# Expert weights loaded two chunks at a time, their low parts written over the raw weights, and the transposes of the gated rows moved

## The chip, the cores and the metric

The kernel runs on 1 core of one Trainium2 chip. The metric is the device time of one execution in microseconds; the median of 3 runs of the kernel before is 2552.89 us (2551.38 to 2554.53). TensorE (PE) multiplies, ScalarE (ACT), VectorE (DVE) and GpSimd (POOL) do element work, and SyncE (SP) issues most of the transfers. Sixteen DMA engines move the data.

## The reference

Two layers over a graph of 625 nodes with 1024 features. Each layer adds a graph product and a kernelized attention to x, then a mixture of experts. The change is in the mixture of experts of the first layer:

```python
def _mlp(h, wg, wu, wd):
    return jax.nn.silu(h @ wg) * (h @ wu) @ wd
...
C = int(np.ceil(CAP_FACTOR * NK / E))          # 98 rows an expert; E = 16, K = 2, F = 1408
expert_inputs = jnp.zeros((E, C, d), x.dtype).at[idx_flat, pos_c].add(x_pair)
expert_outputs = jax.vmap(_mlp)(expert_inputs, w_gate, w_up, w_down)
gathered = expert_outputs[idx_flat, pos_c] * (vals_flat * within)[:, None]
output_tokens = gathered.reshape(N, K, d).sum(axis=1)
return x + _mlp(x, sw_gate, sw_up, sw_down) + output_tokens.reshape(b, s, d)
```

wg and wu are 1024 x 1408 an expert, wd is 1408 x 1024, all in float32. One expert's three matrices are 17.3 MB (3 x 1024 x 1408 x 4 bytes), 16 experts 277 MB. `sw_*` is the shared expert, which all 625 rows pass.

## The kernel before

A float32 product is made of three TensorE products in the type fp32r: every operand is split into a high part (a rounded copy, by ACT, `a_high`) and a low part (what is left, by DVE, `v_low`), and high x high, high x low and low x high are summed in PSUM (`mm_high`, `mm_low`).

The weights come in chunks of 128 rows of the contracted dimension. A chunk of wg or wu is 128 x 1408 (704 KB, rows of 5632 bytes), one of wd, of the shared expert and of all other matrices 128 x 1024 (512 KB). An expert has 8 chunks of wg, 8 of wu and 11 of wd. The list `Weights.all` has all chunks of the program in the order of use, in four regions; region 1 is the experts. Each chunk passes three steps:

1. SP issues its DMA into a raw buffer. Region 1 has five of them, `er0` to `er4`; a buffer is taken again when the low part of the chunk five places before is made (`c.raw_over`, line 733 on).
2. ACT copies it to the high half of a slot, `es0` to `es2`, and DVE makes the low half of the same slot from raw and high. A slot is free when the product of the chunk three places before is done (`a_place`). ACT and DVE work up to three chunks ahead (`due`).
3. TensorE makes its products: for wg and wu three pieces of 512, 512 and 384 columns times three parts, 9 matmuls; for wd two pieces times three parts, 6 matmuls.

`t_experts` sets the order on TensorE. For expert x it is: gate product (`t_up` of wg); the transposes of the gated rows of expert x-1 (`t_turn`, 11 of them); up product (`t_up` of wu); the transposes of the tokens of expert x+1 (`t_enter`, 8 of them); down product of expert x-1 (`t_down`); and for x < 12 one unit of the shared expert (`t_unit`; gate and up units turn 8 weight pieces, down units go block by block). After expert 15 come its transposes, its down product and the last six units. ACT and DVE have matching lists (`a_experts`, `v_experts`). ACT applies silu to the gate product and writes `eg` (line 2041); DVE multiplies it by the up product into `eh` (`v_product`, line 2173), which `t_turn` reads. `a_turned` and `v_turned` split the transposed rows into `heT_h` and `heT_l`.

PSUM has 8 banks, given out in turn (`Banks.take`): the gate product takes 3, the transposes 3, the up product 3, so the up product takes one bank of the gate product of the same expert and waits until silu has read it.

The experts' inputs are scattered to `scr_ei` by POOL (line 2193) and read back expert by expert (`xin`); the outputs go to `scr_eo` (`a_down`), are gathered by POOL after the last expert (line 2211), and DVE adds them to x (`v_combine`). The first chunks of region 1 wait, in `a_place`, for that scatter to land, since their slots lie over rows that it reads.

## Time and profile before

| what | us |
|---|---|
| median of 3 runs | 2552.89 (2551.38 to 2554.53) |
| span of the profiled execution | 2546.2 |
| PE busy | 2453.1 (96%) |
| DVE busy | 1815.8 (71%) |
| ACT busy | 1424.6 (56%) |
| POOL busy | 631.0 (25%) |

The profiled execution has no time of its own beside its span; the median of the runs is 6.7 us over the span, which is what lies around it (start and end of the launch). The experts lie at about 430 to 1315 us. In the page's 40 slices these are the ones in which the DMA engines are 90% busy or more and move 317 to 360 GB/s. A matmul's row says how long it was under way; matmuls overlap, so what a stage costs is read from the starts of its matmuls. The granted TensorE clock is at 9 tenths or more in every slice.

### The profile page before, as it was taken

The page shows a single profiled execution, that of the slowest core. Times are in us where ns is not written, and L with a number is a line of the kernel's source. Part 1 is how long each engine was busy: PE and PEld are TensorE (multiplying, and loading weights), DVE is VectorE, ACT ScalarE, POOL GpSimd, SP SyncE. Part 2 cuts the span into 40 slices and gives each one's busy share as a digit, 9 for nine tenths or more (in the row PEclk, how much of TensorE's full clock was granted, in tenths as well). Part 3 has the DMA queues.
Part 4 walks back from the last instruction along what each step waited for, and adds up shares of the span by engine and source line. Part 5 has one row for each costly group of instructions (what it writes and reads, how often), then busy time and mean ns, then how long its engine had stood idle before and what let it go on. Part 6 is the DMA issues. An engine that isn't in the chain of part 4 may idle for free.

```text
span 2546.2 us, 32572 instructions
## 1 busy us (share of the span) xinstructions
PE 2453.1 (96%) x12692; PEld 2015.9 (79%) x12692; DVE 1815.8 (71%) x2006; ACT 1424.6 (56%) x1890; POOL 631.0 (25%) x538
## 2 busy tenths in 40 slices
PE   7999999999999999999999999999999989999999
PEld 6978798776777777776777778887899987777797
DVE  7449655878787888778868876556666768887453
ACT  5337433766676766667753344443377758885131
POOL 5858215333221000000011004443000006556000
PEclk9999999999999999999999999999999999999999
DMA  5334027999999999999985445444311138885212
GB/s 172 80 100 126 7 83 219 332 334 317 345 321 333 335 326 332 332 341 360 358 272 158 131 132 160 130 125 133 121 58 44 46 110 271 277 280 162 92 55 74
DMA packets 174096, 508.18 MB, mean 200 GB/s; under 512 B 30220, under 2 KB 48025, under 8 KB 173944
## 3 DMA queue, kind: packets, MB, share of 16 engines
q1 hardware_dynamic: 124520, 418.01, 47.3%
q0 software_dynamic: 34928, 74.92, 10.6%
q10 hardware_dynamic: 14496, 13.17, 1.6%
q8 instruction: 101, 1.65, 0.3%
q14 instruction: 51, 0.42, 0.1%
HBM read 458.93 MB, written 46.88 MB: 199 GB/s over the span
## 4 chain that ended last, share of the span: by engine, by line
PE 74%; DVE 12%; DMA 7%; ACT 3%; issue 2%; POOL 1%; SPq 0%; DVEq 0%; ACTq 0%
PE ps L204 72%; DVE es_l L243 4%; DMA er<-in_wd 2%; DVE od L235 2%; ACT es_h L767 1%; DVE Aw L231 1%; DMA gr<-scr_y,gidx 1%; DVE x L231 1%; DMA wk<-in_Wk 1%; DMA scr_ei<-xn,sdi 1%; PE ps L1997 1%; PE ps L1209 1%; DVE eh L231 1%; POOL scr_ei L2193 0%; DVE ws_l L243 0%
## 5 line engine op out<-in xcount | busy, mean ns | idle before, releaser
L243 DVE TENSOR_TENSOR es_l<-er,es_h 128x1408 fp32r<-128x1408 f32 (+1 forms) x455 | 651.8, 1446 | 174.0 <-ACT es_h L767 169.4
L767 ACT ACTIVATE es_h<-er 128x1408 fp32r<-128x1408 f32 (+1 forms) x455 | 562.9, 1242 | 247.8 <-PE ps L204 136.6
L767 ACT ACTIVATE ws_h<-wr 128x1024 fp32r<-128x1024 f32 (+1 forms) x105 | 110.1, 1051 | 205.0 <-PE ps L204 197.0
L243 DVE TENSOR_TENSOR ws_l<-wr,ws_h 128x1024 fp32r<-128x1024 f32 (+1 forms) x103 | 128.6, 1249 | 113.5 <-ACT ws_h L767 113.1
L204 PE MATMUL ps<-es_h,xe_h 128*98 128x512 f32 (+1 forms) x768 | 205.9, 376 | 2.2 <-ACT es_h L767 1.8
L204 PE MATMUL ps<-es_l,xe_h 128*98 128x512 f32 (+1 forms) x768 | 205.4, 376 | 0.8 <-DVE es_l L243 0.2
L204 PE MATMUL ps<-es_h,xe_l 128*98 128x512 f32 (+1 forms) x768 | 204.8, 375 | 0.0
L2199 POOL DMA_DIRECT2D xin<-scr_ei x16 | 9.4, 590 | 627.5 <-PE ps L1969 612.0
L204 PEld LDWEIGHTS ps<-es_l,xe_h 128*98 128x98 f32 x768 | 124.6, 163 | 41.2 <-DVE es_l L243 4.1
L204 PEld LDWEIGHTS ps<-es_h,xe_h 128*98 128x98 f32 x768 | 123.5, 163 | 41.6 <-ACT es_h L767 3.4
L204 PEld LDWEIGHTS ps<-es_h,xe_l 128*98 128x98 f32 x768 | 125.2, 163 | 37.9
L3025 POOL DMA_INDIRECT wrow<-scr_inv,gdst x96 | 110.4, 1150 | 154.6 <-DVE B_l L243 93.1
L2311 POOL DMA_INDIRECT gr<-scr_y,gidx x96 | 122.9, 1280 | 103.2 <-PE ps L204 79.1
L1178 POOL DMA_INDIRECT scr_edges<-dat,idx x85 | 122.6, 1443 | 25.9 <-issue 25.9
L204 PE MATMUL ps<-ws_h,T_h 128*125 128x512 f32 x320 | 127.7, 399 | 0.0
L243 DVE TENSOR_TENSOR T_l<-T,bh 128x1024 fp32r<-128x1024 f32 x64 | 78.2, 1225 | 68.8 <-ACT bh L2823 68.8
L239 DVE SCALAR_TENSOR_TENSOR gl<-gr,gw,gh 128x1024 fp32r<-128x1024 f32 x96 | 120.4, 1279 | 9.1 <-ACT gh L2274 9.0
L204 PE MATMUL ps<-ws_h,T_l 128*125 128x512 f32 x320 | 126.8, 396 | 0.0
L204 PE MATMUL ps<-ws_l,T_h 128*125 128x512 f32 x320 | 126.8, 396 | 0.0
L2274 ACT ACTIVATE gh<-gr,gw 128x1024 fp32r<-128x1024 f32 x96 | 109.9, 1145 | 23.3 <-PE ps L204 13.3
L204 PE MATMUL ps<-es_h,heT_h 128*98 128x512 f32 x352 | 112.8, 402 | 10.3 <-ACT es_h L767 10.2
L204 PE MATMUL ps<-T_h,ws_h 128*128 128x314 f32 x528 | 122.0, 310 | 0.7 <-DVE ws_l L243 0.7
(476 smaller groups left out, 6258.8 us busy)
## 6 DMA issues: line engine op xcount, KB each, us to landing
er<-in_wg SPq DMA_DIRECT2D x128, 704.0 KB, 6.7
er<-in_wu SPq DMA_DIRECT2D x128, 704.0 KB, 6.3
er<-in_wd SPq DMA_DIRECT2D x176, 512.0 KB, 5.2
B<-in_rel SPq DMA_DIRECT2D x64, 512.0 KB, 3.4
scr_y<-y SPq DMA_DIRECT2D x45, 448.0 KB
wr<-in_Wqkv SPq DMA_DIRECT2D x16, 512.0 KB, 5.5
wr<-in_gate SPq DMA_DIRECT2D x16, 512.0 KB, 3.5
wr<-in_w SPq DMA_DIRECT2D x13, 512.0 KB, 3.4
```

Source lines behind the costliest of these rows:

```text
L204: return e.matmul(out, l, r, start=start, stop=stop, skip_group_check=True)
L231: return e.tensor_tensor(out, x, y, op)
L235: return e.tensor_scalar(out, x, s1, s2, op0) if op1 is None else e.tensor_scalar(out, x, s1, s2, op0, op1)
L239: return e.scalar_tensor_tensor(out=out, in0=x, scalar=s, in1=y, op0=op0, op1=op1)
L243: return e.tensor_tensor(lo, src, hi.bitcast(F32), ALU.subtract)
L767: q.e.activation(c.hi, c.at, ACT.Copy).then_inc(*self.s("high").up(c.key))
L1178: q.e.indirect_dma_start(self.d_edges, to, self.m["dat2"][0:TP, 4 * c:4 * c + 4], None).then_inc(*self.landed("edges").up(c))
L1209: ins = e.transpose(ps.one(bs[k // 4], 128, (k % 4) * TP, TP), buf[t][:, k * 128:(k + 1) * 128], self.ident[0:TP, 0:TP])
L1997: ins = q.e.transpose(ps.one(bs[f // 4], 128, (f % 4) * C0, C0), self.m["eh"][0:C0, f * 128:(f + 1) * 128], self.ident[0:C0, 0:C0])
L2274: q.e.activation(m[f"gh{c % NH}"], m[f"gr{c % NR}"], ACT.Copy, scale=m["gw"][:, c:c + 1]).then_inc(*self.s("rows_high").up(c))
L2311: e.indirect_dma_start(m[f"gr{c % NR}"], None, self.d_y[:, :], of).then_inc(*self.landed(f"rows{c % NR}").up(c))
L3025: e.indirect_dma_start(m["wrow"][:, c * 8:(c + 1) * 8], None, self.d_inv[:, :], of).then_inc(*self.landed("row_weights").up(c))
```

## The change

- Two neighbouring chunks of an expert's matrix come in one transfer (`add_two`), from weights laid out so on the host (`by_two`): rows of 11264 bytes for wg and wu and of 8192 bytes for wd, 1408 KB and 1024 KB a transfer. The eleventh chunk of wd comes alone (`wd_last`). The raw buffers `pr0` to `pr4` hold two chunks each.
- The low part is written over the raw chunk (`pr_l` is the same memory). So a raw buffer is taken again only when the products of both its chunks are done. The slots `hs0` to `hs2` hold the high part alone and lie elsewhere; the first use of two of them waits for another thing than before, and no longer for the scatter.
- The transposes of the gated rows of expert x-1 stand in the gate product of expert x, ahead of its fifth chunk (`k == 4`), those of expert 15 in the down product of expert 14, ahead of its ninth chunk. `eh` is gone: DVE multiplies in place in `eg`.
- Expert 15 gets a unit of the shared expert (the 13th of the interleaved ones), so it stands ahead of the last down product, and five units follow the last down product instead of six.
- `eo` is one buffer. All other matrices that were read as two half rows of 2048 bytes are laid out on the host as rows of 4096 bytes (`quarters`, `by_half`); their transfers keep their size.

The diff, cut:

```diff
@@ -161,8 +164,32 @@
         self.of[key] = len(self.all)
         self.all.append(Chunk(key, src, n, region, **how))
 
+    def add_two(self, keys, src, n, region):
+
+        self.add(keys[0], src, n, region, with_it=keys[1:])
+        self.add(keys[1], src, n, region, part=1)
+
+    def place_loads(self, raws, highs):
+
+        mine = [c for c in self.all if c.region == 1]
+        last_in, held, load = {}, {}, -1
+        for i, c in enumerate(mine):
+            if not c.part:
+                load += 1
+                c.raw = raws[load % len(raws)]
+                c.raw_over = last_in.get(c.raw)
+            else:
+                c.raw = raws[load % len(raws)]
+            last_in[c.raw] = c
+            c.slot = highs[i % len(highs)]
+            c.over, held[c.slot] = held.get(c.slot), c
+            at = slice(c.part * c.n, (c.part + 1) * c.n)
+            c.at, c.lo, c.hi = self.m[c.raw][:, at], self.m[c.raw + "_l"][:, at], self.m[c.slot][:, 0:c.n]
+        self.last_in = last_in | held
+
     def place(self, raws, rings):
-        for r in range(4):
+        self.place_loads(raws[1], rings[1])
+        for r in (0, 2, 3):
             mine = [c for c in self.all if c.region == r]
...
@@ -316,10 +338,11 @@
             at(f"wr{i}", W + 16384 + i * 4096, 1024)
         for i in range(KD):
             at(f"wk{i}", R1 + i * 4096, 1024)
-        for i in range(3):
-            pair(f"es{i}", (R1 + 4096, R1 + 15360, W)[i], 1408)
-        for i in range(5):
-            at(f"er{i}", R1 + 26624 + i * 5632 if i < 2 else W + 11264 + (i - 2) * 5632, 1408)
+        for i, o in enumerate((R1 + 4096, R1 + 15360, R1 + 26624, W, W + 11264)):
+            at(f"pr{i}", o, 2 * F0)
+            at(f"pr{i}_l", o, 2 * F0, F32R)
+        for i, o in enumerate((U + 14144, R3 + 26816, W + 22528)):
+            at(f"hs{i}", o, F0, F32R)
 
         for i in range(5):
...
@@ -568,15 +589,16 @@
         u = 14
 
         def downs(e):
-            for f in range(FB):
-                W.add(("wd", e, f), a["wd"][e, f * 128:(f + 1) * 128, :], 1024, 1)
+            for i in range(FB // 2):
+                W.add_two([("wd", e, 2 * i), ("wd", e, 2 * i + 1)], a["wd"][e, i], 1024, 1)
+            W.add(("wd", e, FB - 1), a["wd_last"][e], 1024, 1)
         for e in range(E0):
             for n in ("wg", "wu"):
-                for k in range(KD):
-                    W.add((n, e, k), a[n][e, k * 128:(k + 1) * 128, :], F0, 1)
...
                 self.s_bias(q)
-            if c.raw_over:
+            if c.part:
+                continue
+            if c.raw_over and c.region == 1:
+                q.wait_ge(self.s("product"), c.raw_over.key)
+            elif c.raw_over:
                 q.wait_ge(*self.low(c.raw_over.key))
-            elif c.region == 1 and c.raw in ("er0", "er1"):
+            elif c.region == 1 and c.raw in ("pr0", "pr1", "pr2"):
                 q.wait_ge(self.s("aggregated"), T - 1)
             elif c.region == 1:
                 q.wait_ge(self.s("product"), self.last0)
                 q.wait_ge(*self.low(self.last0))
             elif c.region == 2:
-                q.wait_ge(*self.low(self.last1))
+                for n in {"wr0": ("pr4",), "wr1": ("pr4", "hs2"), "wr2": ("hs2",)}[c.raw]:
+                    q.wait_ge(self.s("product"), self.W.last_in[n].key)
             elif c.region == 3:
                 q.wait_ge(self.s("product"), ("block", 8, 3))
-            dst = c.at.rearrange("p (k c) -> p k c", k=c.src.shape[1]) if len(c.src.shape) == 3 else c.at
-            e.dma_start(dst, c.src).then_inc(*self.landed(c.raw).up(c.key))
+            dst = m[c.raw][:, 0:c.src.shape[1]] if c.region == 1 else c.at
+            e.dma_start(dst, c.src).then_inc(*self.landed(c.raw).up(c.key, *c.with_it))
         ov = self.out.rearrange("(t p) d -> p t d", p=TP)
...
@@ -777,12 +803,13 @@
             q.wait_ge(self.s("summed"), (NW - 1, 1))
         elif c.region == 3:
             q.wait_ge(self.s("product"), ("block", 8, {"ws0": 4, "ws1": 12}[c.slot]))
-        elif c.region == 1 and c.slot != "es2":
-            q.wait_ge(self.s("x_plus_xn"), T - 1)
-            q.wait_ge(self.landed("placed"), 2 * T - 1)
-        elif c.region and c.slot:
-            q.wait_ge(self.s("product"), self.last0 if c.region == 1 else self.last_es2)
-            q.wait_ge(*self.low(self.last0 if c.region == 1 else self.last1))
+        elif c.region == 1:
+            q.wait_ge(self.s("product"), ("swg", 0))
+            if c.slot == "hs2":
+                q.wait_ge(*self.low(self.last0))
+        elif c.region == 2 and c.slot:
...
@@ -1943,17 +1970,14 @@
         u = 14
         for x in range(E0):
             self.t_up(q, "wg", x)
-            if x:
-                self.t_turn(q, x - 1)
             self.t_up(q, "wu", x)
             if x < E0 - 1:
                 self.t_enter(q, x + 1)
             if x:
                 self.t_down(q, x - 1)
-            if x < E0 - 4:
+            if x < E0 - 4 or x == E0 - 1:
                 self.t_unit(q, u)
                 u += 1
-        self.t_turn(q, E0 - 1)
         self.t_down(q, E0 - 1)
         for i in range(u, len(self.units)):
             self.t_unit(q, i)
...
@@ -1977,6 +2001,8 @@
         for j in range(2):
             q.wait_ge(*ps.done(("enter", x), j, "low"))
         for k in range(KD):
+            if n == "wg" and x and k == 4:
+                self.t_turn(q, x - 1)
...
@@ -2005,6 +2031,8 @@
         for j in range(3):
             q.wait_ge(*ps.done(("turn", x), j, "low"))
         for f in range(FB):
+            if x == E0 - 2 and f == 8:
+                self.t_turn(q, E0 - 1)
             c = self.W.all[self.W.of["wd", x, f]]
             L = tuple(self.m["heT_" + j][:, f * C0:(f + 1) * C0] for j in "hl")
...
@@ -2030,34 +2058,36 @@
                     self.a_entered(q, 0, j)
             self.a_unit(q, i)
         u = 14
-        for x in range(E0 + 1):
-            if x < E0:
-                for k in range(KD):
-                    self.a_high(q, ("wg", x, k))
-                for i, (a, b) in enumerate(UPS):
-                    q.wait_ge(self.s("product"), ("wg", x, KD - 1))
-                    if x:
-                        q.wait_ge(*ps.done(("wu", x - 1), 2))
-                    e.activation(m["eg"][0:C0, a:b], ps.one(ps.group["wg", x][i], C0, 0, b - a), ACT.Silu).then_inc(*ps.out(("wg", x), i))
-                for k in range(KD):
-                    self.a_high(q, ("wu", x, k))
-                    if x and k < 3:
-                        self.a_turned(q, x - 1, k)
-            else:
-                for k in range(3):
-                    self.a_turned(q, x - 1, k)
+        for x in range(E0):
+            for k in range(KD):
+                self.a_high(q, ("wg", x, k))
+                if x and k > 4:
+                    self.a_turned(q, x - 1, k - 5)
+            for i, (a, b) in enumerate(UPS):
+                q.wait_ge(self.s("product"), ("wg", x, KD - 1))
+                if x:
+                    q.wait_ge(self.s("turned_hidden"), x - 1)
+                e.activation(m["eg"][0:C0, a:b], ps.one(ps.group["wg", x][i], C0, 0, b - a), ACT.Silu).then_inc(*ps.out(("wg", x), i))
+            for k in range(KD):
+                self.a_high(q, ("wu", x, k))
             if x:
                 for f in range(FB):
                     self.a_high(q, ("wd", x - 1, f))
                     if 3 <= f < 5 and x < E0 - 1:
                         self.a_entered(q, x + 1, f - 3)
+                if x == E0 - 1:
+                    for j in range(3):
+                        self.a_turned(q, x, j)
                 self.a_down(q, x - 1)
             else:
                 for j in range(2):
                     self.a_entered(q, 1, j)
-            if x < E0 - 4:
+            if x < E0 - 4 or x == E0 - 1:
                 self.a_unit(q, u)
                 u += 1
+        for f in range(FB):
+            self.a_high(q, ("wd", E0 - 1, f))
...
-                    if x and k < 3:
-                        self.v_turned(q, x - 1, k)
-            else:
-                for k in range(3):
-                    self.v_turned(q, x - 1, k)
+        for x in range(E0):
+            for k in range(KD):
+                self.v_low(q, ("wg", x, k))
+                if x and k > 4:
+                    self.v_turned(q, x - 1, k - 5)
+            for k in range(KD):
+                self.v_low(q, ("wu", x, k))
             if x:
                 for f in range(FB):
                     self.v_low(q, ("wd", x - 1, f))
-                    if f < 3 and x < E0:
+                    if f < 3:
                         self.v_product(q, x, f)
                     if 3 <= f < 5 and x < E0 - 1:
                         self.v_entered(q, x + 1, f - 3)
+                if x == E0 - 1:
+                    for j in range(3):
+                        self.v_turned(q, x, j)
             else:
                 for i in range(3):
                     self.v_product(q, 0, i)
                 for j in range(2):
                     self.v_entered(q, 1, j)
-            if x < E0 - 4:
+            if x < E0 - 4 or x == E0 - 1:
                 self.v_unit(q, u)
                 u += 1
...
@@ -2168,9 +2199,7 @@
         a, b = UPS[i]
         q.wait_ge(self.s("product"), ("wu", x, KD - 1))
         q.wait_ge(*ps.done(("wg", x), i))
-        if x:
-            q.wait_ge(self.s("turned_hidden"), x - 1)
-        tt(q.e, m["eh"][0:C0, a:b], ps.one(ps.group["wu", x][i], C0, 0, b - a), m["eg"][0:C0, a:b], ALU.mult).then_inc(*ps.out(("wu", x), i))
+        tt(q.e, m["eg"][0:C0, a:b], ps.one(ps.group["wu", x][i], C0, 0, b - a), m["eg"][0:C0, a:b], ALU.mult).then_inc(*ps.out(("wu", x), i))
 
     def v_combine(self, q, t):
...
+        return W.reshape(k, 128, 2, 512).transpose(2, 1, 0, 3).reshape(2, 128, k * 512)
+
+    def by_two(W):
+        e, k, n = W.shape
+        return W.reshape(e, k // 256, 2, 128, n).transpose(0, 1, 3, 2, 4).reshape(e, k // 256, 128, 2 * n)
+
     cst = np.zeros((128, 128 + NT), np.float32)
```

What stands in each engine's program, in the places that matter. First TensorE, expert 3, before: the last chunk's low products of the gate product (`xe` are the expert's rows, `es` the weights' slots), the 11 transposes, the first chunk of the up product.

```order
L204 MATMUL ps<-es_l,xe_h 98x512 [waits low]
L204 MATMUL ps<-es_l,xe_h 98x512
L204 MATMUL ps<-es_l,xe_h 98x384
L1997 MATMUL ps<-cst,eh 128x98 [waits bank3_emptied,bank2_emptied,bank1_emptied]
L1997 MATMUL ps<-cst,eh 128x98 x10
L204 MATMUL ps<-es_h,xe_h 98x512 [waits bank6_emptied,high,bank5_emptied,bank4_emptied]
L204 MATMUL ps<-es_h,xe_h 98x512
```

The same gate product after the change, at its fifth chunk:

```order
L231 MATMUL ps<-pr_l,xe_h 98x512 [waits low]
L231 MATMUL ps<-pr_l,xe_h 98x512
L231 MATMUL ps<-pr_l,xe_h 98x384
L2023 MATMUL ps<-cst,eg 128x98 [waits bank3_emptied,bank2_emptied,bank1_emptied]
L2023 MATMUL ps<-cst,eg 128x98 x10
L231 MATMUL ps<-hs_83,xe_h 98x512 [waits high]
```

And at its end, where the up product follows at once:

```order
L231 MATMUL ps<-pr_l,xe_h 98x512 [waits low]
L231 MATMUL ps<-pr_l,xe_h 98x512
L231 MATMUL ps<-pr_l,xe_h 98x384
L231 MATMUL ps<-hs_81,xe_h 98x512 [waits bank6_emptied,high,bank5_emptied,bank4_emptied]
L231 MATMUL ps<-hs_81,xe_h 98x512
```

The transposes no longer stand between the two products; the up product's wait for `bank6_emptied`, which is a bank of the gate product, is the same.

SP's program in region 1, after the change: the loads of the down product of expert 0, a unit, and the next gate product. Each waits for the product of the second chunk of the pair in its buffer.

```order
L771 DMA pr_71<-in_wd 128x2048 [waits product]
L771 DMA pr_73<-in_wd 128x2048 [waits product]
L771 DMA pr_75<-in_wd 128x2048 [waits product]
L771 DMA pr_77<-in_wd 128x2048 [waits product]
L771 DMA pr_79<-in_wd 128x2048 [waits product]
L771 DMA pr_71<-in_wd_last 128x1024 [waits product]
L771 DMA pr_73<-in_swu 128x1024 [waits product]
L771 DMA pr_75<-in_wg 128x2816 [waits product]
```

Before, each of these was a DMA of one chunk that waited for a low part:

```order
L745 DMA er_78<-in_wd 128x1024 [waits low]
L745 DMA er_79<-in_wd 128x1024 [waits low]
L745 DMA er_80<-in_wd 128x1024 [waits low]
L745 DMA er_81<-in_wd 128x1024 [waits low]
L745 DMA er_77<-in_wd 128x1024 [waits low]
```

A chunk's load thus moved from "low part five chunks back" to "product of a load five loads back". ACT's first three copies of region 1, before:

```order
L767 ACTIVATE es_h<-er_77 128x1024 [waits landed_placed,x_plus_xn,landed_er0]
L767 ACTIVATE es_h<-er_78 128x1024 [waits landed_er1]
L767 ACTIVATE es_h<-er_79 128x1024 [waits low,product,landed_er2]
```

and after:

```order
L793 ACTIVATE hs_81<-pr_71 128x1024 [waits landed_pr0]
L793 ACTIVATE hs_82<-pr_73 128x1024 [waits landed_pr1]
L793 ACTIVATE hs_83<-pr_75 128x1024 [waits low,landed_pr2]
```

The wait for `landed_placed`, the scatter of the experts' inputs, is gone from the first of them.

## Rows read from the trace of the kernel before

**Rows 1.** The page's first line.

```profile
span 2546.2 us, 32572 instructions
```

**Rows 2.** Timeline of PE at edges of stages: start us, us, instruction, [idle <-releaser].

```profile
470.86 0.80 PE L204 MATMUL ps<-es_h,xe_h 128*98 128x512 f32 x3
...
1092.94 0.81 PE L204 MATMUL ps<-es_h,xe_h 128*98 128x512 f32 x3
...
1141.49 0.80 PE L204 MATMUL ps<-es_h,xe_h 128*98 128x512 f32 x3
...
1291.77 1.09 PE L1997 MATMUL ps<-cst,eh 98*128 98x98 f32 x11
1297.55 0.72 PE L204 MATMUL ps<-es_h,heT_h 128*98 128x512 f32 x1 [4.69 <-ACT es_h L767]
...
1314.52 0.53 PE L204 MATMUL ps<-T_h,es_h 128*128 128x314 f32 x2
...
1367.36 0.72 PE L1209 MATMUL ps<-cst,lnx 125*128 125x125 f32 x5 [3.15 <-ACT lnx L1227]
```

**Rows 3.** Timeline of PE, the edges inside the round of expert 5.

```profile
698.41 0.80 PE L204 MATMUL ps<-es_h,xe_h 128*98 128x512 f32 x3
...
713.72 1.09 PE L1997 MATMUL ps<-cst,eh 98*128 98x98 f32 x11
714.62 0.85 PE L204 MATMUL ps<-es_h,xe_h 128*98 128x512 f32 x3
...
729.97 0.84 PE L1969 MATMUL ps<-cst,xin 98*128 98x98 f32 x8
730.59 0.69 PE L204 MATMUL ps<-es_h,heT_h 128*98 128x512 f32 x2
...
747.28 0.53 PE L204 MATMUL ps<-T_h,es_h 128*128 128x314 f32 x2 [0.59 <-DVE es_l L243]
...
754.35 0.81 PE L204 MATMUL ps<-es_h,xe_h 128*98 128x512 f32 x3
```

**Rows 4.** Timeline of PE, second and seventh chunk of a down product.

```profile
675.74 0.63 PE L204 MATMUL ps<-es_h,heT_h 128*98 128x512 f32 x2
...
682.72 0.63 PE L204 MATMUL ps<-es_h,heT_h 128*98 128x512 f32 x2
```

**Rows 5.** Waits, 450 to 1300 us: engine line <- releaser, us, times, longest.

```profile
ACT es_h L767 <- DMA er<-in_wd: 42.6, 61, 2.6
ACT es_h L767 <- DMA er<-in_wg: 28.7, 29, 2.0
...
ACT es_h L767 <- DMA er<-in_wu: 19.7, 30, 1.7
```

**Rows 6.** Windows: stretch, length, busy of PE, PEld, DVE, ACT, POOL, clock, DMA share, GB/s.

```profile
980.40:1036.60 56.20, 55.68 (x279) 42.45 (x278) 45.86 (x40) 38.93 (x38) 0.56 (x1) 1.00 0.93 328
...
1200.00:1212.00 12.00, 12.00 (x64) 9.36 (x63) 10.66 (x7) 9.22 (x10) 0.00 (x0) 1.00 1.01 408
1228.00:1236.00 8.00, 8.00 (x37) 5.64 (x36) 7.76 (x10) 6.44 (x8) 0.00 (x0) 1.00 0.83 296
```

**Rows 7.** Groups, 1400 to 1800 us: what writes a low part over its own input.

```profile
L243 DVE TENSOR_TENSOR B_l<-B,bh 128x1024 fp32r<-128x1024 f32 x44 | 53.9, 1225 | 58.6 <-ACT bh L2823 58.5
```

**Rows 8.** The silu of the same expert as Rows 3: timeline of ACT.

```profile
713.92 1.46 ACT L2041 ACTIVATE eg<-ps 98x512 f32<-98x512 f32 x3 [0.47 <-PE ps L204]
```

**Rows 9.** Timelines of ACT and PE around the first chunks of region 1.

```profile
406.75 2.00 ACT L767 ACTIVATE es_h<-er 128x1024 fp32r<-128x1024 f32 x2 [5.72 <-DMA scr_ei<-xn,sdi]
...
409.20 0.49 PE L204 MATMUL ps<-es_h,hid_h 128*125 128x512 f32 x1 [2.79 <-DVE es_l L243]
...
417.81 0.45 PE L204 MATMUL ps<-T_h,es_h 128*128 128x314 f32 x2
```

**Rows 10.** The chain that ended last, 1330 to 1357 us: start us, us, what.

```profile
1330.60 11.20 DMA yg<-scr_eo,sgi
...
1347.31 1.29 DVE x L239
...
1353.28 3.09 DVE x L231 x5
```

80 lines of the change are left out of this document (41 added, 39 removed).

## The prediction

> **What bounds the kernel now.** I read the page first: the experts fill the slices in which the DMA engines are busiest, PE is 96% busy over the span of 2546.2 us [rows 1]. A busy PE says little, so I went to the starts of the matmuls. Eleven rounds of the expert loop (gate, transposes, up, tokens, down, unit) run from 470.86 to 1092.94: 622.08 us, 56.55 a round. Four rounds without a unit (12 to 15) run from 1092.94 to 1291.77: 198.83 us [rows 2]. Inside one round the gate product takes 15.31 us, the transposes 0.90, the up product 15.35, the tokens 0.62, the down product 16.69, the unit 7.07 [rows 3]. All but one are PE at its pace: gate and up are 72 matmuls at 0.213 us. The down product is not. Five chunks of it that nothing holds up take 682.72 - 675.74 = 6.98 us, 1.396 each, so eleven should take 15.36 [rows 4]. A round without stalls is thus 15.31 + 0.90 + 15.35 + 0.62 + 15.36 + 7.07 = 54.61 us, and 1.94 us a round are lost, 21.4 us over the eleven. A round without a unit is 47.54, four of them (the last has no tokens, minus 0.62) 189.54, so 9.3 us are lost there.
>
> Who causes it: in the waits of this stage ACT's copy `es_h` waited for weights to land 42.6 + 28.7 + 19.7 = 91.0 us, most often, 61 times, for wd [rows 5]. ACT runs up to three chunks ahead, so only a part reaches PE. The DMA engines were 0.93 busy over a round, at 328 GB/s; while they loaded wu they moved 408 GB/s, while they loaded wd 296 GB/s at 0.83 [rows 6]. So they can feed PE (a round's 17.3 MB of expert, 0.5 of unit and about 0.8 of tokens and outputs in 55 us is 338 GB/s), but not in the down product, which eats 524 KB in 1.396 us, 376 GB/s, with only 512 KB transfers that were asked for late.
>
> At the two ends of the stage there are other waits: after round 15 PE turns the last gated rows and then stands, 1297.55 - 1291.77 = 5.78 us for 0.90 us of work [rows 2]; and at the start ACT waited 5.72 us for the scatter of the tokens, and PE 2.79 us behind it [rows 9].
>
> **The change, part by part.**
>
> *Loads and buffers.* A raw buffer was held from issue to the low part; now from issue to the product of its second chunk, but there are ten chunks' room instead of five raw and three slots. The first chunk of a pair is asked for when the product of the chunk nine places before is done, eight products ahead of its own: 8 x 1.396 = 11.2 us in the down product, 8 x 1.91 = 15.3 in gate and up. ACT wants it three chunks before its product, 4.2 us, which leaves 7.0 us for 1024 KB, which are 3.5 us at 296 GB/s [rows 6]. More than before is asked for while the unit runs: by its end the loads of 8 chunks of the next gate are out. So I expect the wait for weights nearly gone: of 1.94 us a round I keep 0.2, of 9.3 us in the last four rounds 1.2 (they have no unit in which the loads catch up). Longer rows move more a busy microsecond; the rows here bound that between nothing and the ratio of 408 at share 1.01 (5632-byte rows) to 296 / 0.83 = 357 (4096-byte rows), 13%; I need none of it, since PE is the limit after this.
>
> The Trainium skill has a rule against this part ("DMA: Bandwidth & Descriptors", section "Where 436 GB/s comes from"): from HBM to SBUF the memory's side binds at about 358 GB/s a core, so longer rows bring nothing. The trace does not agree for a single core in use: 408 GB/s over 12 us [rows 6]. By that rule a round without a unit, 18.1 MB, would take 50.6 us and stay bound by the loads; by the row it takes 44.4 and is not. It is the page's side of the first rival below.
>
> *The low part over the raw chunk.* DVE does the same work on the same sizes. The kernel does this elsewhere: 1225 ns for a 128x1024 in place [rows 7]. Cost nothing.
>
> *The transposes inside the gate product.* Their 0.90 us stays on PE. What they covered does not: the up product needs a bank that silu must have read. The gate product ends at 713.72, silu starts at 713.92 and its three parts take 1.46 us [rows 8]; the up product started at 714.62, 0.90 us after the gate product, and now PE would stand for that time. From below it is 0.20 + a third of 1.46 = 0.69 us, from above 0.90 plus what ACT may be late by (its copies take more than 1 us). I take 0.90, in each of rounds 1 to 15 (round 0 has no transposes and its banks don't meet). In the order the wait for the bank stands unchanged at the up product, and nothing is left in front of it.
>
> Rounds 1 to 11: 54.61 + 0.90 + 0.2 = 55.7, against 56.55: -9.3 us. Rounds 12 to 15: 189.54 + 4 x 0.90, + 0.90 for the transposes of expert 15 that come into round 15, + 1.2 = 195.2, against 198.83: -3.6 us.
>
> *A unit ahead of the last down product.* Before: 5.78 us of transposes and wait, then the down product to 1314.52, 22.75 us from 1291.77 [rows 2]. After: unit 7.07 + down 15.36 = 22.4: -0.3 us. The split of the turned rows lies beside the unit. One unit fewer then follows. I give nothing for it: after the last down product the outputs must land, POOL must gather them, and DVE add them. The sixth gather lands at 1341.80, DVE adds until 1353, then takes the last products [rows 10], and the layer norm's first transposes start at 1367.36, after 3.15 us of wait for ACT [rows 2]. That chain counts from the end of the last down product, 52.84 us, and does not need the six units. PE will be 7 us early and wait. Bounds: 0 and -7.07; I take 0, because DVE went without a break from 1347 on.
>
> *The start.* ACT's first copies no longer wait for the scatter. The idle 2.79 us before 409.20 go, and the second of the two down units took 417.81 - 409.20 = 8.61 instead of 7.07, since DVE was late with the first one's sums: 1.5 more [rows 9, 3]. -4.3 us. Next in line there are the loads of the first gate chunks, wanted 20 us later; they hide.
>
> *The other matrices* keep their transfers' size; PE and DVE bound those stages. Nothing, at most -1.
>
> Sum: -9.3 - 3.6 - 0.3 - 4.3 = -17.5 us. Against the span: 2528.7. The runs lie 6.7 us over the span of the profile, so 2552.9 - 17.5 = 2535.4 us.
>
> **Rivals.**
>
> *The loads stay the limit.* The engines were 0.93 busy already [rows 6]; with the gap added, PE asks later for the same bytes and the stall only moves. For it: at 328 / 0.93 = 353 GB/s a round without unit needs 51.3 us. Against: the 408. Then rounds 12 to 15 gain nothing (+3.6) and half of the 21.4 us stays (+8.5): 2547.5 us.
>
> *The pair comes too late* (the slower side). Its first chunk must wait for the bytes of the second, 1.8 us at 296 GB/s. It decides from where a 1024 KB pair needs over 7.0 us from issue to landing, which it would with one pair queued ahead at 296 GB/s. Then no stall of the loop goes, and the uncovered silu (0.90 x 15) and the moved transposes (0.90) are paid on top: the start gives 4.3 back, the end 0.3: 13.5 + 0.9 - 4.6 = +9.8, 2562.7 us, and more if the stalls grow. Against it: the loads are asked for at a steady pace now and none but the down product is this tight.
>
> *Better than that.* The silu gap is hidden or nearer 0.69, and the unit moved does shorten the tail, or the residual stalls are nil: -3.1, up to -7.1 and -3.4. Two of these three make about 2525 us.
>
> **How the numbers follow.** Forecast 0.64, loads the limit 0.13, pair too late 0.07, better 0.16. A run of this kernel tells 0.2% apart, 5.1 us. Forecast and better are faster, loads the limit is half faster, half the same: faster 0.86, the same 0.07, slower 0.07. The predicted time is the forecast's, 2535.4. The range: down to 2520 (all three of the better ones, nearly), up to 2548 (the loads the limit); the late pair is left out.
>
> **What would show it.** Down products of 15.4 to 15.7 us in all rounds; ACT's waits for the weights' landing from 91 us to under 20; 0.9 us between the last matmul of a gate product and the first of the up product, PE released by ACT `eg`, in rounds 1 to 15; rounds 1 to 11 of 55.7 us; no wait of ACT for `scr_ei` and the two down units in 14.2 us; from the end of the last down product to the layer norm still 52 to 53 us, with PE's stall in the last down units grown by about 7 us. Wrong would make it: down products over 16.5 us (the loads), a gap over 1.5 us (ACT late), or gate products over 17.

## The result, and the profile after

The changed kernel takes 2531.5 us (median of 5 runs, 2529.3 to 2540.2), the kernel before 2551.4 beside it (5 runs, 2547.1 to 2554.5). The ratio is 0.9927, with a 95% interval from 0.9906 to 0.9948: 19.9 us faster by the medians. Two of its five runs took 2539 to 2540 us. The page's first line, against [rows 1] (16.5 us less):

```profile
span 2529.7 us, 32153 instructions
```

The same edges of stages as in [rows 2], and the two waits of PE in the tail, from the timeline of PE (start us, us under way, instruction, [idle before it <-releaser]):

```profile
466.57 0.63 PE L231 MATMUL ps<-hs,xe_h 128*98 128x512 f32 x2
...
1076.67 0.81 PE L231 MATMUL ps<-hs,xe_h 128*98 128x512 f32 x3
...
1271.15 0.46 PE L231 MATMUL ps<-T_h,hs 128*128 128x314 f32 x2
...
1278.11 0.62 PE L231 MATMUL ps<-hs,heT_h 128*98 128x512 f32 x2
...
1293.39 0.45 PE L231 MATMUL ps<-T_h,hs 128*128 128x314 f32 x2
...
1328.67 0.76 PE L231 MATMUL ps<-hs,hid_h 128*125 128x512 f32 x1 [7.25 <-DVE hid_l L270]
...
1336.00 0.47 PE L231 MATMUL ps<-hs,hid_h 128*125 128x512 f32 x1 [2.03 <-DVE pr_l L270]
...
1349.85 0.65 PE L1236 MATMUL ps<-cst,lnx 125*128 125x125 f32 x2 [3.13 <-ACT lnx L1254]
...
1357.11 0.48 PE L231 MATMUL ps<-ws_h,T_h 128*125 128x512 f32 x1
```

| stretch | before | after | difference | predicted |
|---|---|---|---|---|
| to the gate product of expert 1 | 470.86 | 466.57 | -4.3 | -4.3 |
| rounds 1 to 11 | 622.08 | 610.10 | -12.0 | -9.3 |
| rounds 12 to 15 | 198.83 | 194.48 | -4.4 | -3.6 |
| to the end of the last down product | 22.75 | 22.24 | -0.5 | -0.3 |
| to the layer norm's first transposes | 52.84 | 56.46 | +3.6 | 0 |
| from there to the end | 1178.84 | 1179.85 | +1.0 | 0 |

The stretch from the last down product to the layer norm's first transposes is called the tail below.

The waits of the stage from 440 to 1290 us (engine line <- releaser, us in total, times, longest), against [rows 5]:

```profile
ACT hs L793 <- PE ps L231: 176.6, 306, 4.0
...
ACT hs L793 <- DMA pr<-in_wg: 15.3, 13, 1.9
PE ps L231 <- ACT eg L2070: 6.3, 7, 1.0
```

ACT now waits for PE, which is what sets the pace. Of 91.0 us of wait for weights 15.3 are left, none of it for wd or wu. The windows (columns as in [rows 6]): over a whole round the DMA engines move 335 GB/s where it was 328, and in one stretch of 8 us they reach 430:

```profile
970.00:1025.00 55.00, 54.11 (x276) 42.12 (x275) 42.93 (x37) 39.26 (x39) 0.55 (x1) 1.00 0.89 335
1228.00:1236.00 8.00, 8.00 (x47) 6.36 (x46) 6.91 (x6) 5.60 (x5) 0.00 (x0) 1.00 1.02 430
```

### The profile page after: what moved, and what is told of

It reads as the page before. It is cut to its first block, busy times and chain, and to the rows that moved or that the text cites. A ratio compares the mean times of both kernels' runs of the same rounds, so it can differ in the third digit from the quotient of the medians.

```text
span 2529.7 us, 32153 instructions
## 1 busy us (share of the span) xinstructions
PE 2438.7 (96%) x12692; PEld 2018.9 (80%) x12692; DVE 1814.5 (72%) x2006; ACT 1425.8 (56%) x1890; POOL 645.0 (25%) x538
## 4 chain that ended last, share of the span: by engine, by line
PE 83%; DVE 9%; issue 3%; DMA 2%; ACT 2%; POOL 0%; SPq 0%; DVEq 0%; ACTq 0%; POOLq 0%
PE ps L231 82%; DVE od L262 2%; DVE Aw L258 1%; DMA gr<-scr_y,gidx 1%; DVE x L258 1%; DVE ua L258 1%; DMA wk<-in_Wk 1%; DMA yg<-scr_eo,sgi 1%; PE ps L2023 1%; PE ps L1236 1%; DVE ws_l L270 1%; DVE zq_l L270 0%; ACT ws_h L793 0%; DVE gl L266 0%; PE ps L1993 0%
## 5 line engine op out<-in xcount | busy, mean ns | idle before, releaser
L270 DVE TENSOR_TENSOR pr_l<-pr,hs 128x1408 fp32r<-128x1408 f32 (+1 forms) x455 | 649.9, 1446 | 146.9 <-ACT hs L793 144.5
L793 ACT ACTIVATE hs<-pr 128x1408 fp32r<-128x1408 f32 (+1 forms) x455 | 562.3, 1241 | 214.5 <-PE ps L231 187.6
L231 PE MATMUL ps<-hs,xe_h 128*98 128x512 f32 (+1 forms) x768 | 206.3, 377 | 12.2 <-ACT eg L2070 6.3
L270 DVE TENSOR_TENSOR ws_l<-wr,ws_h 128x1024 fp32r<-128x1024 f32 (+1 forms) x103 | 128.7, 1250 | 113.3 <-ACT ws_h L793 108.8
L231 PE MATMUL ps<-pr_l,xe_h 128*98 128x512 f32 (+1 forms) x768 | 204.9, 375 | 0.0
L231 PE MATMUL ps<-hs,xe_l 128*98 128x512 f32 (+1 forms) x768 | 204.6, 375 | 0.0
L231 PEld LDWEIGHTS ps<-hs,xe_h 128*98 128x98 f32 x768 | 122.8, 163 | 52.9 <-issue 17.7
L231 PEld LDWEIGHTS ps<-pr_l,xe_h 128*98 128x98 f32 x768 | 125.2, 163 | 37.9
L231 PEld LDWEIGHTS ps<-hs,xe_l 128*98 128x98 f32 x768 | 125.1, 163 | 38.0
L1205 POOL DMA_INDIRECT scr_edges<-dat,idx x85 | 140.8, 1657 | 25.9 <-issue 25.9
L231 PE MATMUL ps<-T_l,ws_h 128*128 128x314 f32 x528 | 120.8, 308 | 0.0
```

Of the source, the lines that this page charges most:

```text
L231: return e.matmul(out, l, r, start=start, stop=stop, skip_group_check=True)
L270: return e.tensor_tensor(lo, src, hi.bitcast(F32), ALU.subtract)
L793: q.e.activation(c.hi, c.at, ACT.Copy).then_inc(*self.s("high").up(c.key))
L1205: q.e.indirect_dma_start(self.d_edges, to, self.m["dat2"][0:TP, 4 * c:4 * c + 4], None).then_inc(*self.landed("edges").up(c))
```

## The experiments

All twelve are edits of the changed kernel, except the last. Each is compared with the kernel before on its own chip; its medians beside these runs are 2551.4, 2552.4, 2554.3 and 2553.7 us, so different occasions differ by up to 3 us. A ratio's interval is some 0.2% (5 us) to either side. A profile is one execution and need not be typical; where its time is far from the median, it stands beside it.

### Four pairs instead of five

```diff
-        raw, rawe = [f"wr{i}" for i in range(3)], [f"pr{i}" for i in range(5)]
+        raw, rawe = [f"wr{i}" for i in range(3)], [f"pr{i}" for i in range(4)]
```

> The changed kernel with four buffers for pairs instead of five; rows as long as in the changed kernel. Theory (room): a pair is now asked for six products ahead instead of eight, 6 x 1.396 = 8.4 us in the down product, of which ACT's lead takes 4.2 and leaves 4.2 us for 1024 KB that take 3.5 us and the way to landing: the wait for weights comes back, 1 to 2 us a round, 15 to 30 us slower than the changed kernel, 0.998 to 1.004 of before. Rival (row length is what counts): within 3 us of the changed kernel, 0.992 to 0.993.

Measured: 2557.39 us, ratio 1.0024 (1.0010 to 1.0038). The whole gain is gone, with every other edit still in place. The waits for weights are back, from 440 to 1290 us:

```profile
ACT hs L793 <- DMA pr<-in_wg: 59.4, 25, 5.5
ACT hs L793 <- DMA pr<-in_wd: 20.9, 21, 1.9
ACT hs L793 <- DMA pr<-in_wu: 5.3, 8, 1.4
```

What follows: the room, and with it the lead of the requests (eight to nine products ahead, with four pairs six to seven), is what removed the stalls. No run has ten single buffers instead of five pairs, so the pairing by itself was not tested.

### Pairs without the long rows

```diff
-            e.dma_start(dst, c.src).then_inc(...)
+            e.dma_start(dst[:, 0:c.n], c.src[:, 0:c.n]).then_inc(...)
+            e.dma_start(dst[:, c.n:2 * c.n], c.src[:, c.n:2 * c.n]).then_inc(...)
```

> The changed kernel, but each pair of chunks comes in two transfers with half rows (5632 and 4096 bytes instead of 11264 and 8192), into the same buffers, asked for at the same times; both halves must land as before. Theory (room and early requests took the wait for weights away, not the long rows): the down products stay at 15.3 to 15.5 us and the time within 2 us of the changed kernel, 0.992 of before. Rival (long rows made the loads fast enough): ACT waits for weights again, down products of 16.5 us and more, 10 to 20 us slower than the changed kernel, 0.996 to 1.000.

Measured: 2531.37 us, ratio 0.9925 (0.9901 to 0.9949), as the changed kernel. Down products take 15.3 us, but for one of 15.88. In this kernel the length of a row (4096 and 5632 bytes against 8192 and 11264) is worth nothing.

### The other matrices again in half rows

```diff
-                W.add(("W0", h, i), a["W0"][h, i], 1024, 0)
+                W.add(("W0", h, i), W2(a["W0"][h, i]), 1024, 0)     # and rel, root, Wout, gate
```

> The changed kernel, with the matrices outside the experts and shared units (W0, rel, root, Wout, gate) loaded again as two rows of 2048 bytes a partition instead of one of 4096. Theory (PE and DVE bound those stages): no difference, 2530 to 2533. Rival (their long rows are part of the 3.6 us by which the changed kernel came in under the forecast): 2 to 4 us slower, 2534 to 2536, with the relations' stage after the layer norm longer by that much.

Measured: 2532.46 us, ratio 0.9915 (0.9895 to 0.9935). No difference that can be told.

### One bank of silu at a time

```diff
-        for emptied in ps.before((n, x)):
-            q.wait_ge(*emptied)
+        for i in range(2 if n == "wu" else 3):
+            for emptied in ps.before((n, x), i):
+                q.wait_ge(*emptied)
...
+            if n == "wu" and k == 0:   # four matmuls into two banks, then the wait for the third, then its two
```

> The changed kernel, with one wait of TensorE moved: the first chunk of an up product multiplies its first two pieces (four matmuls, 0.85 us) before it waits for the bank of the third piece, which is the one that silu reads. My theory: in the changed kernel PE stands 0.84 to 1.08 us between gate and up product in 15 rounds, since the transposes that covered the silu are gone; here the gap falls to under 0.3 us in each round, and the time by about 15 x 0.85 = 12.8 us, to about 2519 us (0.987 of the kernel before). Rival: the gap is only slack, since the weights or the split of the chunks set the pace of a round; then the down products grow by the same amount and the time stays at 2529 to 2533 us (0.992).

Measured: 2519.03 us, ratio 0.9872 (0.9852 to 0.9891); the profiled execution took 2514.7. The gap between the gate and the up product of one expert, in the timelines of PE and ACT (columns as in [rows 3, 8]), of the changed kernel:

```profile
704.13 0.80 PE L231 MATMUL ps<-pr_l,xe_h 128*98 128x512 f32 x3
705.66 0.85 PE L231 MATMUL ps<-hs,xe_h 128*98 128x512 f32 x3 [0.73 <-issue]
...
704.34 0.40 ACT L2122 ACTIVATE heT_h<-ps 128x294 fp32r<-128x294 f32 x1
704.97 1.46 ACT L2070 ACTIVATE eg<-ps 98x512 f32<-98x512 f32 x3 [0.23 <-PE ps L231]
```

and of this one:

```profile
751.15 0.66 PE L231 MATMUL ps<-hs,xe_h 128*98 128x512 f32 x2
751.65 0.62 PE L231 MATMUL ps<-hs,xe_l 128*98 128x512 f32 x2
...
751.35 1.46 ACT L2077 ACTIVATE eg<-ps 98x512 f32<-98x512 f32 x3 [0.23 <-PE ps L231]
```

In the first PE starts the up product when silu's first part is through (704.97 + 0.6), in the second it runs on. Gate and up product meet in one bank, the one that silu's first part reads, and it is the up product's third matmul that needs it. The edit does two things: it splits the wait, and it puts four matmuls (0.85 us: the first two pieces, with the high and with the low part of the rows) ahead of the third piece, which would otherwise be reached after two. The medians give 12.5 us, 0.83 for each of 15 experts. The traces say the same from another side: in the changed kernel the up product starts 1.07 to 1.31 us after the gate product's last matmul, in 15 places, which without the usual step of 0.23 makes 13.7 us in all; in this kernel no step inside gate and up is over 0.45 us. No run puts the transposes back where they had covered the silu.

### The unit back behind the last down product

```diff
-            if x < E0 - 4 or x == E0 - 1:      # in PE's, ACT's, DVE's and the loads' order
+            if x < E0 - 4:
```

> The changed kernel with the 13th interleaved unit back behind the last down product (six units follow it, as before the change). Theory of the prediction: what follows the last down product is set by outputs landing, gathers and DVE, 52.8 to 56.5 us from its end, with five or six units alike. Then the last down product ends about 7.0 us earlier, less some 2 us in which it waits for its rows to be split behind the down product of expert 14, and the whole is about 5 us faster than the changed kernel: 2526 us (0.990). Rival: TensorE's work sets the tail, and the moved unit only changes places: 2531 to 2534 us (0.992 to 0.993), with the wait for the split rows as the loss.

Measured: 2532.49 us, ratio 0.9925 (0.9906 to 0.9943). My theory gave 2526, and the gain of 5 us that it needs is not in the medians (2531.37 for the short rows on the same chip). In its profile (2528.5 us) PE stands 2.53 us before the last down product (DVE `heT_l` is late), and then runs with a granted clock of 0.66 over 1271 to 1276 us, so the product ends 4.2 us late and not 2. The tail takes 57.48 us, with all six units behind the last down product, as in the kernel before (52.84). So the moved unit is worth nothing that these runs can tell, and it isn't what made the tail longer.

### The start: the wait for the scatter put back

```diff
             q.wait_ge(self.s("product"), ("swg", 0))
+            q.wait_ge(self.s("x_plus_xn"), T - 1)
+            q.wait_ge(self.landed("placed"), 2 * T - 1)
```

> The changed kernel, with the wait put back that ACT had before its first copies of the experts' weights: for the scatter of the tokens and for x + xn. Theory (the start gave what the trace shows, two down units in 13.97 us instead of 18.55): they take about 18.5 us again, ACT shows a wait for scr_ei of 4 to 6 us near 407 us, and the time is 4.3 us longer than the changed kernel's 2531.5, about 2536 (ratio 0.994 to before). Rival (the start was given back by loads of the first gate product that came late): the first gate and up product of the loop get shorter by what the units lose, and the time stays at 2531 to 2532.

Measured: 2544.94 us (2533.6 to 2553.3), ratio 0.9968 (0.9952 to 0.9984). The median is 13 us over the changed kernel's where 4.3 were expected. PE and ACT at that place:

```profile
413.25 0.79 PE L231 MATMUL ps<-hs,hid_h 128*125 128x512 f32 x1 [6.04 <-DVE pr_l L270]
...
410.88 2.95 ACT L793 ACTIVATE hs<-pr 128x1024 fp32r<-128x1024 f32 x3 [9.05 <-DMA scr_ei<-xn,sdi]
```

ACT waits 9.05 us, where it was 5.72 [rows 9], since the scatter lands later: 18.8 us after its last issue, where it was 15.5. The two down units take 21.9 us, 7.9 more than in the changed kernel: PE stands 6.04, and the other 1.9 are matmuls at a granted clock of 0.62 (over 413 to 418 us). These 7.9 us are all that the profile shows, whose execution took 2539.1 us; the rest of the 13 in the median is not explained. That the scatter lands later was new; several of the experiments below look at it.

### DVE's first additions behind the last up unit

```diff
             self.v_unit(q, i)
-            if i == end - 4:
+            if i == end - 3:
                 for t in range(3):
                     self.v_combine(q, t)
```

> The changed kernel, with DVE's six first additions of gathered rows (combine 0 to 2) moved behind the last up unit's hf and hid_l, so that PE's last down units don't wait for them. Theory A (after the last down product DVE's own chain sets the end: gathers land, ten additions, then the additions of the last products): PE's idle 7.25 us before the last down units go, but the layer norm starts only 1 to 3 us earlier, 2529 to 2530.5. Rival B (PE's last down units, 18 us from hid_l on, set the end): 5 to 7 us earlier, 2525 to 2526.5. Rival C (the ring of seven gather buffers: the gathers 7 to 9 wait for the additions that are now late): up to 2 us later, 2532 to 2534.

Measured: 2540.79 us (2536.8 to 2554.3), ratio 0.9951 (0.9934 to 0.9967). Slower, and by more than any of the three theories gave. Its profiled execution took 2554.3 us, 13.5 over the median, and its trace shows two separate causes. One is the edit: the layer norm starts 60.8 us after the last down product, against 56.5. PE's wait for `hid_l` went, but a longer one came, for the low part of the next weights, which DVE also computes behind the additions, and POOL waited 8.2 us for the ring of gather buffers, as rival C has it:

```profile
1354.09 0.76 PE L231 MATMUL ps<-hs,hid_h 128*125 128x512 f32 x1 [15.47 <-DVE pr_l L270]
```

The other lies 900 us earlier, where this kernel is the same as the changed one. Its waits from 400 to 440 us:

```profile
POOL xin L2228 <- DMA scr_ei<-xn,sdi: 31.7, 1, 31.7
...
PE ps L1993 <- DMA xin<-scr_ei: 8.1, 1, 8.1
```

The timeline of PE there, and two windows behind it (after POOL's busy time comes the granted clock):

```profile
430.71 1.54 PE L1993 MATMUL ps<-cst,xin 98*128 98x98 f32 x8 [8.05 <-DMA xin<-scr_ei]
```

```profile
430.00:434.00 4.00, 3.29 (x16) 3.32 (x17) 1.04 (x2) 1.71 (x3) 3.08 (x4) 0.50 0.06 2
...
441.00:451.00 10.00, 10.00 (x49) 7.70 (x48) 8.44 (x7) 7.47 (x7) 8.18 (x8) 1.00 0.88 294
```

The tokens' scatter landed 31.7 us after its last issue; in the changed kernel's profile it was 18.2, in the one before 15.5. PE stood 8.05 us for `xin`, and after that its granted clock was 0.50 (1.2 GHz), so the eight transposes took 1.25 us instead of 0.62 and the next unit 9.1 instead of 7.1.

### The gathers' source moved

```diff
-        self.ei = nc.dram_tensor("scr_ei", (E0 * C0 + 2 * N, D), F32).ap()
+        self.ei = nc.dram_tensor("scr_ei", (E0 * C0 + 2 * N + 1111, D), F32).ap()
```

> The changed kernel, with the DRAM tensor ahead of scr_eo made 4.55 MB longer, so that the experts' outputs, from which the tokens are gathered after the last down product, lie elsewhere in the memory. Rows of the two profiles: packets of the gathers took 265 ns (median) in the changed kernel and 191 ns before, on the same bytes, and the sixth gather 16.91 us against 11.20. Theory (where the tensor lies, since the weights' new layout moved it, makes the gathers slower): their median changes to near 191 ns and the stretch from the last down product to the layer norm from 56.5 to near 53 us. Rival (it is what else runs at that time, or one execution's chance): 250 ns and 56 us as they are, 2531.5.

Measured: 2538.72 us (2533.7 to 2548.1), ratio 0.9940 (0.9918 to 0.9961), slower than either theory gave. Counted over the 1250 packets of 4096 bytes that the ten gathers fetch, the median packet took 229 ns here, 269 in the changed kernel and 202 in the one before (the expectation has 265 and 191); the tail took 53.9 us. Halfway between the two theories; see the last experiment. What the profile (2548.1 us) showed instead is the late scatter once more: landed 30.4 us after the last issue, and the matmuls behind it at half the clock. This kernel computes and orders all as the changed one, so the long landing probably belongs to the changed kernel too, in some of its executions; in its one profile the scatter landed after 18.2 us.

### The first pair of gate weights after the scatter

```diff
             if c.part:
                 continue
+            if c.key == ("wg", 0, 0):
+                q.wait_ge(self.landed("placed"), 2 * T - 1)
```

> The changed kernel, with one wait added on the SP queue: the first pair of expert 0's gate weights is asked for only when the scatter of the tokens has landed. In two profiles of kernels with the changed kernel's start the last tokens were still on their way when the first pairs came (issued at 408.7 and 409.3), the scatter landed 31.7 and 30.4 us after its last issue instead of 15 to 19, PE stood 8.1 us for xin, and the next matmuls ran at half the clock; the runs of these kernels spread from 2533 to 2548. Theory (pairs on the queues stretch the scatter's last packets): now the scatter lands 15 to 19 us after its last issue, PE's wait for xin is gone, and the median is 2530 to 2533 with no run over 2538. Rival 1 (the spread is the chip's, as the kernel before shows one too): median 2535 to 2540 and runs over 2545 remain. Rival 2 (the pairs are now late for the first gate product): the gate product of expert 0 is over 18 us long and the time 2 to 4 us more.

Measured: 2534.61 us (2532.3 to 2538.8), ratio 0.9929 (0.9906 to 0.9951). The scatter landed 17.9 us after the last issue, PE did not stand, gate and up product of expert 0 took 30.63 us as in the changed kernel (rival 2 is out), and its six runs spread over 6.5 us where seven of the moved source, on another chip, had 14.4. But the profiled execution is the shortest of the six (2532.3), eleven runs of the kernel before on this chip spread over 18 us, the median is 1.6 us above what I expected and one run took 2538.8: neither the theory's numbers nor those of rival 1. For the mechanism, the transfers of the kernel with DVE's moved additions, where the scatter landed late, 410 to 424 us (queue: packets, MB, share):

```profile
q1 hardware_dynamic: 433, 4.35, 83.0%
q0 software_dynamic: 37, 0.08, 1.5%
...
pr<-in_wg SPq DMA_DIRECT2D x2, 1408.0 KB
```

In these 14 us the pairs (q1) had 433 packets of up to 11264 bytes and the scatter's queue 37. The same from 416.3 to 426 us:

```profile
q1 hardware_dynamic: 256, 2.51, 75.1%
q0 software_dynamic: 27, 0.00, 0.2%
```

The trace's packets, one by one: the scatter's last packet of 4096 bytes ended at 416.07 us. What remained were 27 packets of 4 bytes, 9 ns each, and of the 26 steps from one to the next eleven were 0.42 to 0.43 us, five 0.55 to 0.79 and the rest 0.01, the last packet at 424.6. A packet of 11264 bytes took 422 ns (median). So beside the pairs the queue's small packets passed about one for each packet of a pair. That is not the whole cause: the pairs are asked for 17.1 us after the scatter's last issue in the changed kernel, with the waits by bank, with four pairs and with the wait put back as well, some 3 to 4 us before the scatter landed, and there it landed after 18.2 to 19.4 us. What makes the difference is open.

### The third load later

```diff
-            elif c.region == 1 and c.raw in ("pr0", "pr1", "pr2"):
+            elif c.region == 1 and c.raw in ("pr0", "pr1"):
```

> The changed kernel, with the third transfer of the expert stage (512 KB of in_swu, asked for at 378.4 beside the tokens' scatter) held back to 406 as in the kernel before. Theory (these 512 KB push the scatter's end back by 512 KB at 280 GB/s = 1.9 us, past the first pairs): the scatter lands about 15.5 us after its last issue as before (18.2 in the changed kernel), ahead of the pairs, no long landing, median 2530 to 2534. The cost: ACT's first copies of that unit wait up to 1 us. Rival (the third load has no part in it): the landing stays at 18 to 31 us, with runs over 2545.

Measured: 2536.46 us (2532.4 to 2542.2), ratio 0.9931 (0.9907 to 0.9954). The scatter landed 14.7 us after the last issue, as early as before and 3.5 us earlier than in the changed kernel. That does not show that the third load delays it: with the third load in its early place the scatter landed after 14.8 us in the kernel with half rows, 15.1 with the short rows and 16.6 with the unit moved back. ACT waited 8.9 us for `in_swu`, where up to 1 was expected, and the time is not better.

### Both repairs

> The changed kernel with both repairs: PE waits for each bank of silu by itself before the up product's first matmul into it (which gave 12.5 us alone), and the first pair of gate weights is asked for only when the scatter has landed. Theory (they are independent): 12 to 12.5 us under the run with the second repair alone, 2517 to 2520, with no run over 2525. Rival (the second only shifts the load): as the first repair alone, 2519 with runs up to 2526, or over 2520.

Measured: 2523.09 us (2514.5 to 2525.7), ratio 0.9872 (0.9848 to 0.9897), the same ratio as the waits by bank alone, and 11.5 us under the kernel with the held pairs alone on the same chip: the gain of the waits adds. The second repair gives nothing that the median shows, and the time is the rival's (over 2520), not the theory's. The scatter landed somewhat late here without any pair beside it:

```profile
POOL xin L2237 <- DMA scr_ei<-xn,sdi: 21.5, 1, 21.5
PE ps L1995 <- DMA xin<-scr_ei: 2.1, 1, 2.1
```

### The kernel before, once more

> The kernel before, unchanged, for a second profile of its end: from the end of the last down product to the layer norm's first transposes its first profile has 52.84 us, and nine profiles of kernels with the changed loads 53.9 to 60.8. Theory (the change makes the gathers fly longer, by something in the loads' layout or placement): 52 to 53.5 us again, median gather packet 185 to 200 ns. Rival (one execution's luck): 54 to 57 us, packets over 220 ns.

Measured: 2559.69 us, one execution. The tail took 54.95 us (1322.48 to 1377.43), the median gather packet 229 ns, against 52.84 and 202 in the first profile of the same kernel: the rival's numbers.

## Why the prediction was right, and where it was off

**The loads.** Right in mechanism and size. The round of expert 5 (start times of PE's matmuls) is now gate and up product 7.67 + 23.90, transposes 0.87, tokens 0.62, down product 15.34, unit 7.00. Expert 0, which has no gap, takes 30.63 us for gate and up; of the 0.94 more here 0.84 are the gap. Down products take 15.3 us in every round (15.36 predicted). Four pairs bring the stalls back (though now most for wg, and not for wd), short rows none, so it is the lead, as the step of the eight products said. The 0.2 us a round that I kept for remaining stalls were zero, and so were most of the 1.2 us of the last four rounds: that is 2.2 of the 2.7 us between -12.0 and -9.3, and the -4.4 against -3.6.

The window at 1228 us has 430 GB/s with a single core at work, and [rows 6] had 408. The Trainium skill ("DMA: Bandwidth & Descriptors", section "Where 436 GB/s comes from") lets the memory's side bind at about 358 GB/s a core between HBM and SBUF; the trace disagrees, and by that rule the first rival would have come true. The same section also names a transfer of 16 MB at 425 GB/s, and that agrees with the trace.

**The silu gap.** Right: 0.84 us in the round shown (1.07 from the gate product's last matmul to the up product's first, and 0.23 without the gap), 0.92 in the mean of 15, 0.90 predicted, 12.5 us over the kernel by experiment. I had named the cause and left the cure out: PE waits for three banks where its first matmuls need two. It was the dearest part of the change and could be avoided.

**The end of the loop.** Right in sum (-0.5 against -0.3). The experiment on the moved unit says that it is worth nothing that can be told either way.

**The tail.** The step that gave it at 0 measured +3.6 us. The chain of waits of the changed kernel has, against [rows 10]:

```profile
1307.37 16.91 DMA yg<-scr_eo,sgi
...
1329.80 1.29 DVE x L266
...
1335.77 3.09 DVE x L258 x5
```

The sixth gather flies 16.91 us, not 11.20. Part of the 3.6 us is one execution's luck: the kernel before has 52.84 and 54.95 us in its two profiles. Eleven profiles with the changed loads (the one with DVE's order changed left out) have 53.5 to 58.1, mean 55.9. Whether the remaining 2.0 us between the means are the change's is open; row length, the moved unit and the source's place didn't settle it. The forecast that the moved unit does not shorten the tail held, and PE's 7.25 us of wait in its last down units is as forecast. Of the 1.0 us behind the tail, 0.85 lie in the layer norm's transposes (7.26 us, from 1349.85 to 1357.11, against 6.41): the first sixteen took 3.24 us instead of 2.18, at a granted clock of 0.65 over 1349.8 to 1353.8.

**The start.** The size is right: -4.3 us (two down units in 13.97 us against 18.55, no wait for the scatter). The reason given for 1.5 of them is not. I took the second down unit to be long because DVE was late. The windows of both kernels (columns as in [rows 6]) say that it was TensorE's clock:

```profile
409.00:414.00 5.00, 4.80 (x14) 3.80 (x15) 5.00 (x8) 1.06 (x1) 4.09 (x4) 0.66 1.03 371
...
405.00:414.00 9.00, 9.00 (x42) 7.28 (x41) 6.84 (x11) 0.25 (x1) 3.22 (x4) 1.00 0.72 278
```

In the kernel before, the granted clock after PE's idle 2.79 us was 0.66 in the mean of 5 us, and single matmuls of the second down unit took 0.63 us instead of 0.40; in the changed kernel PE doesn't stand and the clock is full. A wait taken away gave back its own length and the slow matmuls behind it. The page's slices are 64 us long and don't show such a stretch.

The claim behind the start, that nothing is next in line, failed in part: with the wait gone the scatter can matter at `xin`, where PE stood 8 us for it, and in 2 of the 12 profiles with these loads (the late scatters above) it cost some 11 us there (from the down units to the first gate product 39.6 us instead of 28.7). I had looked at the gate chunks and not at the tokens.

**The sum.** By the two spans -16.5 us against -17.5. That it is so close is partly luck: the loop and its end gave 3.7 us more than forecast, the tail and what follows cost 4.6. The median, 2531.5, lies 3.9 us under the forecast. My step from span to median was wrong, here and in the part on time and profile: I took 6.7 us as lying around the span. Every run since has 1.8 to 1.9 us there (2531.5 against 2529.7), so the profiled execution of the kernel before was 4.9 us faster than its median, which is chance. With 1.8 the same sum would have forecast 2530.5.

**The rivals.** Loads stay the limit, and the pair comes too late: both refuted by the down products. "Better than that" was half true (no residual stalls, but the gap in full and no shorter tail).

## What to carry to other kernels

When a stream of loads stalls its consumer though the DMA engines have time to spare, count how many products ahead a load is asked for before touching its size: one pair of buffers less cost 26 us here (2557.4 against 2531.4 us), half the row length nothing. Where an operation that covered a wait is moved, look at what the wait really needs; waiting bank by bank, with four matmuls put ahead of the last bank, gave 12.5 us, the best of all versions (0.9872 of the time before). A wait of TensorE of 2.5 to 8 us mostly cost more than its length here, since the matmuls behind it ran at a lower clock; price both. And a wait that is removed is worth checking in several executions, since what it had held apart can now collide.

## What the hardware showed unexpectedly

- A scattered write whose last packets meet large transfers can land late: 30.4 and 31.7 us after its last issue, in two executions in which the pairs were issued at 409.3 and 408.7; 14.7 to 21.5 in the other twelve profiles, four of which had pairs asked for 3 to 4 us before the landing. In one of the two late ones the last packets, of 4 bytes, passed at about one for each 422 ns packet of a pair. That the pairs cause the lateness is likely, and not shown by the medians.
- TensorE's granted clock mostly fell after waits of a few us: after 8.05 us without work it was 0.50, after 7.25 us (the tail of the changed kernel) 0.59 over 1328 to 1333, after 2.53 us (the unit moved back) 0.66 over 1271 to 1276, after 2.79 us (the kernel before) 0.66 over 409 to 414, where single matmuls took 0.63 us instead of 0.40. One wait did not do it: ahead of the layer norm PE stood 3.15 us in the kernel before and the clock stayed at 1.00 (1367 to 1371), and 3.13 us at the same place in the changed kernel and it was 0.65 (1349.8 to 1353.8). The gaps of 0.8 to 1.1 us between gate and up product left it at 1.00 (480 to 1290 us).
- The same gathers' packets took between 202 and 269 ns (medians) from one execution to another, and 202 and 229 in two executions of one kernel.
